# Spreading the scan input over the partitions by a TensorE product, with three drive banks, in a fused convolution, state-scan and attention kernel

## The reference

```
xz = group_norm(x) @ in_proj_w.T; xh, z = split(xz)          # 96 channels each
xc = silu(depthwise_conv3x3(xh) + conv_b)
xs = 4 directions of xc: rows, columns, and both reversed    # (B, 4, 96, 256)
dts, Bs, Cs = split(x_proj_w[k] @ xs[k])                     # 12, 16 and 16 rows
dts = softplus(dt_projs_w @ dts + dt_projs_b)
for each position t:                                         # 16 states n per channel c
    h[c,n] = h[c,n] * exp(dts[c,t] * A[c,n]) + (dts[c,t] * xs[c,t]) * Bs[n,t]
    y[c,t] = sum_n h[c,n] * Cs[n,t]
y = sum of the 4 directions + Ds * xs
out = (layer_norm(y) * silu(z)) @ out_proj_w.T
```

## Time and profile before

| | |
|---|---|
| median of 3 runs | 397.6 us (397.46 to 617.52) |
| profiled execution | 396.75 us |
| its span | 395.0 us |
| granted TensorE clock, mean | 0.988 |
| busy, PE / DVE / ACT / POOL | 371.8 / 285.2 / 212.7 / 192.4 us |
| transfers | 61.85 MB, 157 GB/s mean |

### The profile page before, as it was taken

One profiled execution on the slowest core, in us unless ns is written; L12 is line 12 of the kernel. 1 busy time (PEld: TensorE's weight loads), 2 busy tenths in 40 slices (PEclk: granted clock), 3 DMA queues, 4 the chain that ended last, 5 costly groups with the idle time before them and its releaser, 6 DMA issues.

```text
span 395.0 us, 7870 instructions
## 1 busy us (share of the span) xinstructions
PE 371.8 (94%) x2805; PEld 288.6 (73%) x2805; DVE 285.2 (72%) x477; ACT 212.7 (54%) x553; POOL 192.4 (49%) x236
## 2 busy tenths in 40 slices
PE   7998969999999999999999999999999999999990
PEld 5878847787797775777767877767586668888770
DVE  4734887999689898999979989799793500553464
ACT  2576447567445574744855657836754431257530
POOL 5222673788187676579665725854362400210021
PEclk9999998999999999999999999999999999999996
DMA  5703999999979999988988996369910000000010
GB/s 115 138 19 100 239 263 254 255 284 262 232 176 256 243 241 264 248 212 223 252 189 222 248 240 171 92 189 253 246 49 1 2 0 2 0 22 2 1 42 20
DMA packets 26240, 61.85 MB, mean 157 GB/s; under 512 B 6935, under 2 KB 10969, under 8 KB 26201
## 3 DMA queue, kind: packets, MB, share of 16 engines
q1 hardware_dynamic: 26201, 61.35, 62.6%
HBM read 57.15 MB, written 4.19 MB: 155 GB/s over the span
## 4 chain that ended last, share of the span: by engine, by line
PE 77%; DVE 9%; DMA 5%; ACT 4%; issue 2%; POOL 1%; SPq 1%; POOLq 0%; ACTq 0%; DVEq 0%
PE ring L1235 15%; PE y_acc L1401 6%; PE ring L1524 5%; PE y_acc L1235 5%; PE ring L1518 5%; DMA in_rep<-step_rows 4%; DVE state L1066 3%; PE b_bc L1376 3%; PE y_acc L1395 3%; PE ring L1445 2%; PE ring L1469 2%; PE ring L1598 2%; PE ring L1535 2%; PE ring L1415 2%; PE ring L1428 2%
## 5 line engine op out<-in xcount | busy, mean ns | idle before, releaser
L586 POOL TENSOR_TENSOR outp<-state,c_rep 128x512 f32<-128x512 f32 x96 | 123.4, 1301 | 62.5 <-PE y_acc L1401 30.2
L1066 DVE TENSOR_TENSOR_SCAN state<-decay,drv 128x512 f32<-128x512 f32 x96 | 117.2, 1220 | 13.6 <-ACT decay L763 6.4
L763 ACT ACTIVATE decay<-in_rep,a_neg 128x255 f32<-128x255 f32 x192 | 86.1, 500 | 54.3 <-DMA in_rep<-step_rows 45.7
L1235 PEld LDWEIGHTS ring<-ident 128*128 128x128 f32 x726 | 90.8, 193 | 23.5 <-issue 15.9
L1235 PE MATMUL ring<-ident 128*128 128x128 f32 (+1 forms) x726 | 99.2, 281 | 4.1 <-ACT room_h L678 2.9
L1055 DVE TENSOR_TENSOR drv<-in_rep,b_bc 128x512 f32<-128x512 f32 x96 | 66.4, 692 | 10.7 <-PE b_bc L1376 2.0
L601 POOL TENSOR_SCALAR mv<-mv 128x2 f32<-128x2 f32 x16 | 4.6, 287 | 82.0 <-DVE mv L1080 81.5
L1401 PE MATMUL y_acc<-outp,band 128*32 128x256 f32 x192 | 33.8, 610 | 0.0
L1235 PE MATMUL y_acc<-ident 128*32 128x128 f32 (+1 forms) x236 | 30.9, 276 | 0.0
L1235 PEld LDWEIGHTS y_acc<-ident 128*32 128x32 f32 (+1 forms) x236 | 24.3, 118 | 5.5 <-issue 5.2
L1524 PE MATMUL ring<-kvw,tT 96*128 96x480 f32 (+1 forms) x52 | 22.9, 567 | 0.0
(11 more groups left out here) (339 smaller groups left out, 622.4 us busy)
## 6 DMA issues: line engine op xcount, KB each, us to landing
in_rep<-step_rows SPq DMA_DIRECT2D x96, 512.0 KB, 6.5
c_rep<-c_rows SPq DMA_DIRECT2D x16, 256.0 KB, 6.1
step_rows<-step SPq DMA_DIRECT2D x8, 384.0 KB, 4.8
x_tok<-in_x_dram SPq DMA_DIRECT2D x4, 192.0 KB, 3.7
out_dram<-res SPq DMA_DIRECT2D x4, 192.0 KB, 2.0
room_a<-in_L_attn_w_qkv_dram SPq DMA_DIRECT2D x1, 432.0 KB, 6.5
c_rows<-step SPq DMA_DIRECT2D x8, 32.0 KB, 6.4
room_h<-in_L_conv_in_proj_w_dram SPq DMA_DIRECT2D x1, 144.0 KB, 4.9
```

The source lines that it names most:

```text
L586: g.tensor_tensor(outp[:, u % SLOTS, :], state[:, u % STATE_SLOTS, :], c_rep[:, part, :], ALU.mult).then_inc(S["outp"], 1)
L763: ins = a.activation(decay[:, back, u % DECAY_SLOTS, e, kept], in_rep[:, slot, 0, :].rearrange("p (e l) -> p e l", e=WAYS)[:, e, kept], AC ...
L1066: v.tensor_tensor_scan(state[:, u % STATE_SLOTS, :][:, order], held[:, order], drv[:, :][:, order], 0.0, ALU.mult, ALU.add).then_inc(S["st ...
L1235: t_.matmul(dst[:, 0:wide], ident[:, 0:cols], ident[:, 0:wide], start=True, stop=True)
```

## The change

The input rows (dt times x) no longer go through memory. They stay in a tile `inp` of 96 channels by 512, two of them in turn, and PE spreads them over the partitions: `broadcast(u)` multiplies `inp` by `pick[:, g, :]`, a 96x128 matrix of ones and zeros that POOL builds once, into `drv[u % 3]`, one of three drive banks (the two `b_bc` banks and the old `drv`). DVE multiplies the bank in place by `b_rep`, B rows that SP loads repeated from memory just as C rows are. PE issues the product for unit u+2 (`LEAD`) ahead of the turn of unit u, and waits for scan u-1 first. `d{n}` now gives B and C rows together, and `keep_c` stores both. `fill_b` and `w_b` go. The store of the step rows waits for `sp_max`, not for the product with x, and the step loads no longer wait for `drive`. PE's wait for the copies of `fq`, `fk`, `fv`, which stood in `scores` together with a filler place, is now at the end of step `fv`.

The side lists, `BANKS` and `FILLERS` are all new; the numbers in `FILLERS` sum to 513 before and 386 after (ahead of and with `d0` 47 and 56, in the stretch of the units 352 and 230, behind it 70 and 80, at key -1 behind `d0` 44 and 20).

```diff
 IN_SLOTS = 4
 DECAY_SLOTS = 2
+DRIVE_SLOTS = 3
+LEAD = 2
...
-NO_PRODUCT = {"conv0", "conv1", "b0", "b1"}
+NO_PRODUCT = {"conv0", "conv1"}
...
-    37: "w_f2.0 q1.0 q2.0 kv00.0 kv01.0", 40: "kv10.0 d.5", 43: "kv11.0 b0.4 cx.0", 49: "b1.4 yT.1 at.0 aT.0", 52: "gT.1 o.1",
...
+    74: "aT.1 s0.0", 76: "p.1", 77: "fv.0", 79: "gT.2 t0.0 s1.0 o.2 t1.0", 80: "hT.1", 82: "w.0", 84: "lg.1",
...
-        step_rows = nc.dram_tensor("step_rows", [2, DI, 2 * TOK], F32, kind="Internal").ap()
-        c_rows = nc.dram_tensor("c_rows", [2, PARTS, SN, TOK], F32, kind="Internal").ap()
-        b_bc = [ctx.enter_context(nc.psum_tensor(f"b_bc{i}", [P, TOK], F32)) for i in range(PARTS)]
-        drv = ctx.enter_context(nc.psum_tensor("drv", [P, TOK], F32))
+        step_rows = nc.dram_tensor("step_rows", [2, DI, TOK], F32, kind="Internal").ap()
+        bc_rows = nc.dram_tensor("bc_rows", [2, 2, PARTS, SN, TOK], F32, kind="Internal").ap()
+        drv = [ctx.enter_context(nc.psum_tensor(f"drv{i}", [P, TOK], F32)) for i in range(DRIVE_SLOTS)]
         y_acc = ctx.enter_context(nc.psum_tensor("y_acc", [P, TOK], F32))
         banks = [ctx.enter_context(nc.psum_tensor(f"ring{i}", [P, TOK], F32)) for i in range(RING)]
-        banks += b_bc + [drv, y_acc]
+        banks += drv + [y_acc]
...
-        in_rep = sb("in_rep", [P, IN_SLOTS, 2, TOK])
-        pre_w = sb("pre_w", [DI, DIRS, DI + NS])
-        w_b = sb("w_b", [DI, DIRS, PARTS, P])
+        b_rep = sb("b_rep", [P, PARTS, TOK])
+        step_rep = sb("step_rep", [P, IN_SLOTS, TOK])
+        pre_w = sb("pre_w", [DI, DIRS, DI + 2 * NS])
+        pick = sb("pick", [DI, GROUPS, P])
...
-        step2 = sb("step2", [DI + NS, 2, TOK])
+        step2 = sb("step2", [DI + 2 * NS, TOK])
+        inp = sb("inp", [DI, 2, TOK])
...
-                sp.dma_start(c_rows[n % 2].rearrange("i s t -> (i s) t"), step2[DI:, 0, :]).then_inc(S["c_kept"], 16)
+                sp.dma_start(bc_rows[n % 2].rearrange("k i s t -> (k i s) t"), step2[DI:, :]).then_inc(S["c_kept"], 16)
+
+            def repeat_b(n, i):
+
+                sp.wait_ge(S["c_kept"], 16 * (n + 1))
+                if n:
+                    sp.wait_ge(S["drive"], UNITS * (n - 1) + GROUPS * (i + 1))
+                sp.dma_start(b_rep[:, i, :], bc_rows[n % 2, 0, i].unsqueeze(0).to_broadcast([GRP, SN, TOK])).then_inc(S["b_there"][i], 16)
...
-                sp.wait_ge(S["step"], n + 1)
+                sp.wait_ge(S["sp_max"], n + 1)
                 if n >= 2:
                     sp.wait_ge(S["decay"], UNITS * (n - 1))
-                sp.dma_start(step_rows[n % 2], step2[0:DI, :, :].rearrange("p a t -> p (a t)")).then_inc(S["step_kept"], 16)
+                sp.dma_start(step_rows[n % 2], step2[0:DI, :]).then_inc(S["step_kept"], 16)
...
-                    sp.wait_ge(S["drive"], u - IN_SLOTS + 1)
                 rows = step_rows[n % 2, GRP * g:GRP * (g + 1), :]
-                sp.dma_start(in_rep[:, u % IN_SLOTS, :, :].rearrange("p a t -> p (a t)"),
-                             rows.unsqueeze(1).to_broadcast([GRP, SN, 2 * TOK])).then_inc(S["in_there"][u % IN_SLOTS], 16)
+                sp.dma_start(step_rep[:, u % IN_SLOTS, :],
+                             rows.unsqueeze(1).to_broadcast([GRP, SN, TOK])).then_inc(S["in_there"][u % IN_SLOTS], 16)
 
             keep_c(0)
             keep_step(0)
+            repeat_b(0, 0)
             for u in range(2):
                 repeat_step(u)
-            for i in range(PARTS):
-                repeat_c(0, i)
+            repeat_c(0, 0)
+            repeat_b(0, 1)
+            repeat_c(0, 1)
...
+            for low in (True, False):
+                pool.wait_ge(S["pick"], 1 if low else 2)
+                g.affine_select(out=pick[:], in_=pick[:], pattern=[[-P if low else P, GROUPS], [-1 if low else 1, P]], compare_op=ALU.is_ge, fill=0.0,
+                                base=SN - 1 if low else 0, channel_multiplier=SN if low else -SN).then_inc(S["pick"], 1)
...
+                if n >= 2:
+                    pool.wait_ge(S["inp_there"], UNITS * (n - 1))
+                g.tensor_tensor(inp[:, n % 2, :], step2[0:DI, :], xs[:, n // PER_IMAGE, :, :].rearrange("p e l -> p (e l)"),
...
+                    act.wait_ge(S["step"], n)
...
-                _, _, part, c16 = unit(u)
-                slot = u % IN_SLOTS
+                part = unit(u)[2]
+                at = drv[u % DRIVE_SLOTS]
                 if u % GROUPS == 0:
-                    dve.wait_ge(S["b_there"], PARTS * (u // UNITS) + part + 1)
-                dve.wait_ge(S["in_there"][slot], 16 * (u // IN_SLOTS + 1))
-                if u:
-                    dve.wait_ge(S["state"], u)
-                v.tensor_tensor(drv[:, :], in_rep[:, slot, 1, :], b_bc[part][:, :], ALU.mult).then_inc(S["drive"], 1)
+                    dve.wait_ge(S["b_there"][part], 16 * (u // UNITS + 1))
+                dve.wait_ge(S["inp_there"], u + 1)
+                v.tensor_tensor(at[:, :], at[:, :], b_rep[:, part, :], ALU.mult).then_inc(S["drive"], 1)
...
-            def fill_b(n, part):
-
-                if n:
-                    pe.wait_ge(S["drive"], UNITS * (n - 1) + GROUPS * (part + 1))
-                i = n // PER_IMAGE
-                pe.wait_ge(S["xs"], i + 1)
-                for e in range(WAYS):
-                    k = WAYS * (n % PER_IMAGE) + e
-                    ins = t_.matmul(b_bc[part][:, e * L:(e + 1) * L], w_b[:, k, part, :], xs[:, i, e, :], start=True, stop=True)
-                ins.then_inc(S["b_there"], 1)
+            def broadcast(u, lead):
+
+                n, g = u // UNITS, unit(u)[3]
+                if u % UNITS == 0:
+                    pe.wait_ge(S["step"], n + 1)
+                if u >= DRIVE_SLOTS:
+                    pe.wait_ge(S["state"], u - DRIVE_SLOTS + 1)
+                t_.matmul(drv[u % DRIVE_SLOTS][:, :], pick[:, g, :], inp[:, n % 2, :], start=True, stop=True).then_inc(S["inp_there"], 1)
...
-                if r == 0:
-                    fill_in(f"s0.{n}", banks_[0])
-                    for w in "qkv":
-                        taken(pe, f"f{w}_{n}")
...
+                    for w in "qkv":
+                        taken(pe, f"f{w}_{n}")
...
-            for part in range(PARTS):
-                fill_b(0, part)
             pe.wait_ge(S["const2"], CONST2)
             pe.wait_ge(S["ones"], ONES)
+            pe.wait_ge(S["pick"], 3)
             for item in pe_side[0]:
                 side(*item)
+            for u in range(LEAD):
+                broadcast(u, 0)
             for u in range(SLOT_COUNT):
+                if u + LEAD < SLOT_COUNT:
+                    broadcast(u + LEAD, LEAD)
```

More of the change, by code:

```diff
@@ L337, in hybrid_kernel @@
         one_of = sb("one_of", [P, 2, 2, HD])
-        gn_banks = [b_bc[0], b_bc[1], drv, y_acc]
+        gn_banks = drv + [y_acc]
         S = {n: sem("s_" + n) for n in (
@@ L342, in hybrid_kernel @@
             "gn_turned gn_stats gn_agg gn_dev gn_var gn_eps gn_rsqrt gn_bias xn padded z_kept gate_e gate_s conv conv_e taps minus_cb xs0 xs "
-            "a_exp raw c_kept step_kept b_there sp_t sp_s sp_l sp_max sp_in sp_exp sp_ln step decay drive state outp y_mm y_ev "
+            "a_exp raw pick c_kept step_kept inp_there sp_t sp_s sp_l sp_max sp_in sp_exp sp_ln step decay drive state outp y_mm y_ev "
             "stat_y agg_y eps_y rsqrt_y neg_y shift_y norm_y gate_w gate_m gate stat_t agg_t eps_t rsqrt_t neg_t shift_t norm_t ctx_lo a_rec att "
@@ L350, in hybrid_kernel @@
         S["c_there"] = [sem(f"s_c_there{i}") for i in range(PARTS)]
+        S["b_there"] = [sem(f"s_b_there{i}") for i in range(PARTS)]
         S["in_there"] = [sem(f"s_in_there{i}") for i in range(IN_SLOTS)]
@@ L479, in side @@
                     keep_step(n)
+                elif step[0] == "b":
+                    repeat_b(n, int(step[1]))
                 else:
@@ L654, in _ @@
             src = bank("w_xp")[0:DI, 0:DIRS * XROWS].rearrange("p (k r) -> p k r", k=DIRS)
[L655 to L657 removed]
+            evac("w_xp", (pre_w[:, :, DI:], src[:, :, RANK:]))
             evac("w_dt", (dtT[:].rearrange("p a b -> p (a b)"), bank("w_dt")[0:RANK, 0:DIRS * DI]))
@@ L737, in pre_raw @@
                     act.wait_ge(S["c_kept"], 16 * n)
+                    act.wait_ge(S["step"], n)
                 for e in range(WAYS):
                     k = WAYS * (n % PER_IMAGE) + e
-                    ins = a.activation(step2[0:DI, 0, e * L:(e + 1) * L], bank(f"d{n}")[0:DI, e * L:(e + 1) * L], ACT.Identity,
+                    ins = a.activation(step2[0:DI, e * L:(e + 1) * L], bank(f"d{n}")[0:DI, e * L:(e + 1) * L], ACT.Identity,
                                        bias=dtb[:, k:k + 1])
                 ins.then_inc(S["raw"], 1)
-                a.copy(step2[DI:, 0, :], bank(f"d{n}")[DI:DI + NS, :]).then_inc(freed(f"d{n}"), 1)
+                a.copy(step2[DI:, :], bank(f"d{n}")[DI:, :]).then_inc(freed(f"d{n}"), 1)
             def pre_softplus(n):
@@ L763, in expo @@
```

(11 more changed lines are left out.)

20 lines of the change are left out of this document (7 added, 13 removed), and 83 rows, old and new, of tables (ACT_SIDE, DVE_SIDE, FILLERS, PE_SIDE).

## The result

| | before | changed |
|---|---|---|
| median | 399.5 us (397.5 to 401.4, one run at 617.5) | 444.0 us (442.0 to 450.7) |
| ratio | | 1.112, 95% interval 1.100 to 1.124 |
| second set of runs | 396.6 us | 444.8 us, ratio 1.120 (1.117 to 1.124) |

The change is slower by 44 to 48 us. Some executions of one kernel show a lower granted clock behind the scans and take a few us more (450.7 us here: last scan at 335.1 us as in the others, 7.7 us more behind it), and the ratios leave them out.

A forecast was written before the change was run, and what follows sets the result against it. PE's in-order list was taken as the bound: span 395.0 + 38.3 (82.6 - 13.8 - 30.5) + 10 for the drive banks = 443.3 us; with 1.75 for the execution and 0.85 for the median, 446 us, range 428 to 466.

The forecast's parts named there:

- PE bounds, by its list: Whole kernel: PE executes one list in order, 5 us of gaps in the scan stretch; its length sets the time, chance 0.85.
- +82.6 us for the broadcasts, at 0.86 us: PE list: one 96x128 by 512-column product for each of 96 units, 0.86 us each, adds 82.6 us.
- -13.8 us for `fill_b`: PE list: `fill_b` goes, 8 scans x 2 parts x 2 products of 0.43 us, saving 13.8 us.
- -30.5 us for fillers: PE list behind `d0`: 136 fewer filler products at 0.224 us, saving 30.5 us.
- The sum of the list by stretches: PE list priced by rows: 250.6 us old, 278.0 new between first and last `y_acc` batch; behind it 86.7 and 92.3.
- +10 us for the ring of drive banks: Scan stretch: PE and DVE wait for each other over three drive banks, adding 10 us, with 0 and +25 as ends.
- The groups of three units: Scan stretch: the longer of PE's and DVE's work per group sums to 294.7 us, 15 more than PE alone.
- How much the lockstep can cost: Scan stretch: PE and DVE at most about three units apart; coupling priced +10 us, ends 0 and +25.
- The loads count nothing: Unit loads halve, 512 to 256 KB, and the first scan starts at 41 to 42 us, but all this is worth 0.
- Rival 1: Scan stretch: a broadcast holds up the next product only 0.22 us, DVE sets the pace, 385 us; chance 0.03.
- Rival 2: Whole kernel: nothing moves beyond 2%, as PE holds 38 us of slack the windows don't show; 398 us, chance 0.03.
- Rival 3: Scan stretch: PE and DVE stall by turns (+25 us) and PE's clock falls in the gaps; 471 us, chance 0.09.

## Why the prediction was right, point by point

The forecast was 446 us, with 428 to 466 as its range; 444.0 and 444.8 were measured. For the span it was 395.0 + 48.3 = 443.3, and the profile has 441.4, or 46.4 more than before.

- *PE bounds, by its list.* Shown: the time grew by 31 us when PE's busy time in the scans grew by 32.7 in the old kernel, and shrank when work was taken from the new one in three different ways (24, 25 and 18 us). In the changed kernel itself the scans take 41.9 us longer, and PE is busy for 39.9 of them.
- *+82.6 us for the broadcasts, at 0.86 us.* The rows shown have 0.86 to 0.90 each, all undisturbed groups 0.91 in the mean. The price by columns was 6% low, or 5 us in all.
- *-13.8 us for `fill_b`, -30.5 us for fillers.* The price of 0.22 us a filler holds where it fills all 128 output rows (174.45 to 174.67). Ahead of a `y_acc` batch the first two cost next to nothing; there were 45 such fillers in the stretch of the units and now are 37, so by an estimate 1.8 us of the 30.5 were never there. The sum of the list by stretches can be held against the trace. Between first and last batch it said 278.0 us against 250.6 for the old list, +27.4; the trace has 283.8 (57.78 to 341.59) against 248.2, +35.6. Ahead of the first batch the list said +5.3, the trace has +4.9. Behind the last batch it said +5.6; the trace has 99.8 against 93.9, +5.9.
- *+10 us for the ring of drive banks.* The difference in the middle stretch, 35.6 - 27.4 = 8.2 us, is what this term had to cover. Only 3 us of it are idle time of PE (8.3 against 5.1). The dearer broadcasts are 5 more (96 x 0.05) and the fillers 1.8; that is 10, as near as such a sum goes (it was 2.4 us off for the old list). So the term's size came out by luck: its mechanism was mostly not the one named, since PE rarely waited, and an under-priced product made up for it. That 446 lies 2 us from the measured time owes something to this. The groups of three units, taking the longer of PE and DVE, gave 294.7 us for 93 units; from first to last scan it is 292.7 for 95.
- *How much the lockstep can cost* I priced as 0 to +25 around +10 and expected 6 us at most for another lead. It was 10 us. Its worth depends on which engine waits.
- *The loads count nothing.* Right: ACT's waits for loads are gone without any gain. The start came a little late, with PE's broadcast as the last to be ready: it ends at about 41.5 (forecast 39.5), and the first scan starts at 42.5 (forecast 41 to 42).
- *Rival 1 (broadcasts cheap, DVE sets the pace).* Excluded by the starts. The spacing that the Trainium skill gives in "TensorE: Matmul & The Clock Gate", "Back-to-back issue gap" for 512 columns, 131 ns sustained, was met by no record here: 430 ns and more at 32 bit, and some 215 ns (178.19 to 178.40) for the 16-bit ones, which is that section's own figure for an isolated product (518 cycles at 512 columns, 216 ns at the upper level).
- *Rival 2 (nothing moves)* asked for PE slack. The weight-load share of TensorE fell to 64% while the kernel got slower. The Trainium skill, in "Perfetto Trace Analysis", "Identifying the Most-Contended Engine", takes that share as a measure of the headroom; the trace disagrees here. A record of a broadcast holds up the next by 430 ns and more, and its weight load takes 189 ns.
- *Rival 3 (clock and lockstep)* didn't come. The mean granted clock is 0.988 in both profiles, and PE's weight loads for broadcasts waited 10.8 us for scans. The clock fell where I took PE work out, fillers above all (0.942) but also half of the broadcasts' work (0.967 and 0.977).

## What to carry to other kernels

Price what a change adds to the engine that runs one full list, by start-to-start rows of the nearest shapes, before counting what it relieves elsewhere: a transfer that halves is worth little while another engine is the bound; here ACT's 45.7 us of waits for loads went and no time was won. Filler products stand in that list like any other work; when real work is put into it, count them, and try the old kernel with fewer of them first. Price them where they stand: those that run beside other products cost less. Where two engines pass banks to each other, place the wait so that the engine that is the bound doesn't make it; here one step of lead cost 10 us.
